# Row gathers of 128 instead of 125 table rows in the last phase of a four-layer graph network

## The reference

```python
out_deg = clip(zeros(n).at[src].add(1), 1)          # edges that leave a node
in_deg  = clip(zeros(n).at[dst].add(1), 1)          # edges that arrive at it
h       = features * (out_deg ** -0.5)[:, None]
agg     = zeros_like(features).at[dst].add(h[src])  # gather by src, add up by dst
return agg * (in_deg ** -0.5)[:, None]
```

## Time and profile before

| | |
|---|---|
| median of 3 runs | 4507.49 us |
| lowest and highest run | 4498.54 and 4508.41 us |
| the profiled execution's own time | 4501.9 us |
| its span, first to last instruction | 4500.1 us |
| busy share of the span: PE (TensorE matmul) | 97% |
| DVE (VectorE) | 91% |
| POOL (GpSimd) | 73% |
| ACT (ScalarE) | 72% |
| `l3` steady stretch, in the span | about 3855 to 4485 us |

### The profile page before, as it was taken

One profiled execution on the slowest core, in us unless ns is written; L12 is line 12 of the kernel. 1 busy time (PEld: TensorE's weight loads), 2 busy tenths in 40 slices (PEclk: granted clock), 3 DMA queues, 4 the chain that ended last, 5 costly groups with the idle time before them and its releaser, 6 DMA issues.

```text
span 4500.1 us, 107824 instructions
## 1 busy us (share of the span) xinstructions
PE 4356.4 (97%) x30591; PEld 3250.0 (72%) x30591; DVE 4096.3 (91%) x11848; ACT 3221.3 (72%) x5358; POOL 3273.1 (73%) x2516
## 2 busy tenths in 40 slices
PE   7999999999998999999999999999999998999998
PEld 5777777777775777777767777777777776666666
DVE  7999999999997999999979999997999998888888
ACT  5777777777774777777757777776777776677777
POOL 6788888888883777777747766765767675777776
PEclk8999999999999999999999999999999999999999
DMA  2111111111112322222211111111111111111111
GB/s 59 28 17 18 18 17 18 17 18 17 18 17 56 84 61 61 61 61 62 61 42 27 28 27 27 28 25 41 28 26 28 27 27 24 31 30 30 30 30 26
DMA packets 339795, 152.11 MB, mean 34 GB/s; under 512 B 250726, under 2 KB 325394, under 8 KB 339754
## 3 DMA queue, kind: packets, MB, share of 16 engines
q0 software_dynamic: 104000, 59.31, 10.3%
q1 hardware_dynamic: 235754, 92.30, 8.2%
HBM read 138.66 MB, written 10.00 MB: 33 GB/s over the span
## 4 chain that ended last, share of the span: by engine, by line
PE 87%; DVE 6%; issue 4%; ACT 1%; DMA 1%; DVEq 0%; another core or an unknown queue 0%; POOL 0%; SPq 0%; POOLq 0%; ACTq 0%
PE acc L664 40%; PE rows_ps L832 17%; PE rows_ps L759 8%; PE bank L759 6%; PE bank L848 5%; PE rows_ps L671 3%; PE eaT_ps L840 3%; PE rows_ps L747 2%; PE rows_ps L668 1%; PE eaT_ps L735 1%; DVE stationary L1325 1%; DVE raw L1349 1%; DVE one_hot L1297 1%; DVE rows_ps L1415 1%; ACT stack L1010 0%
## 5 line engine op out<-in xcount | busy, mean ns | idle before, releaser
L664 PE MATMUL acc<-one_hot,stationary 125*128 125x392 bf16 x12000 | 2334.9, 329 | 51.3 <-DVE stationary L1325 28.4
L648 POOL DMA_INDIRECT gathered<-table_l,row_numbers x1200 | 1598.6, 1332 | 449.8 <-issue 336.9
L664 PEld LDWEIGHTS acc<-one_hot,stationary 125*128 125x128 bf16 x12000 | 1150.8, 99 | 726.0 <-DVE stationary L1325 40.4
L951 ACT ACTIVATE distances<-count_hi,fields 125x392 bf16<-125x392 f16 (+1 forms) x2500 | 1223.1, 558 | 0.0
L1325 DVE TENSOR_TENSOR stationary<-mask,parts 125x1024 bf16<-125x1024 bf16 x1500 | 943.7, 683 | 0.0
L936 ACT CAST mask<-is_lo 125x1024 bf16<-125x1024 f32 x500 | 521.8, 1044 | 485.1 <-issue 293.3
L648 POOL DMA_INDIRECT fields_all<-table_l,row_numbers x500 | 645.8, 1292 | 257.4 <-issue 123.8
L1297 DVE TENSOR_SCALAR one_hot<-count_hi,fields 125x392 bf16<-125x392 f16 x2300 | 738.3, 343 | 13.6 <-issue 13.5
L1415 DVE COPY_PREDICATED rows_ps<-near_bits_now,rows_ps 125x320 f32<-125x320 int8 (+3 forms) x1600 | 580.7, 363 | 181.6 <-PE rows_ps L832 126.7
L648 POOL DMA_INDIRECT gathered<-table_l2a,row_numbers x400 | 511.5, 1279 | 263.3 <-DVE parts L1307 118.8
L648 POOL DMA_INDIRECT gathered<-table_l2b,row_numbers x400 | 511.2, 1278 | 241.3 <-DVE parts L1307 119.3
(11 more groups left out here) (220 smaller groups left out, 4704.0 us busy)
## 6 DMA issues: line engine op xcount, KB each, us to landing
near_key<-near_keys_by_chunk SPq DMA_DIRECT2D x300, 122.1 KB
gathered<-table_l,row_numbers POOLq DMA_INDIRECT x1200
fields<-edge_fields SPq DMA_DIRECT2D x500, 31.2 KB
near_key<-near_keys_by_chunk SPq DMA_DIRECT2D x100, 91.6 KB
fields_all<-table_l,row_numbers POOLq DMA_INDIRECT x500
gathered<-table_l2a,row_numbers POOLq DMA_INDIRECT x400
gathered<-table_l2b,row_numbers POOLq DMA_INDIRECT x400
ea<-in_edge_attr SPq DMA_DIRECT2D x100, 62.5 KB
```

Source lines behind the costliest of these rows:

```text
L648: pool.indirect_dma_start(out=gathered[ph][:, s, t, :], in_=table[ph], out_offset=None, in_offset=bass.IndirectOffsetOnAxis(ap=row_numbers ...
L664: mm = pe.matmul(acc[:, :], stationary[:, s, k, t, :, :].rearrange("p a b -> p (a b)"), one_hot[:, s, t, :], start=first and t == 0 and k ...
L951: ins = act.activation(distances[:, i * n:(i + 1) * n], count_hi[:, 0:n], ACT.Abs, scale=-1.0, bias=fields[:, s, k, t:t + 1].bitcast(F32))
```

## The change

The constant ROWS goes from 125 to 128. That alone only declares `row_numbers`, the gather buffers and `fields_all` with three more partitions and clears 128 partitions of `row_numbers` instead of 125. The gather then takes `rows` partitions: 128 in `l3`, 125 (EP) in the other four phases. The three further row numbers of each `l3` gather are zero, since the loader still writes only 125, so they bring row 0 of the table to partitions 125 to 127 of `gathered2`, which no instruction reads. The number of instructions on each engine and their order stay the same.

```diff
-ROWS = 125
+ROWS = 128
...
                     pool.sem_inc(ev("chunks_begun"), 1)
+                    rows = ROWS if ph == "l3" else EP
                     for t in range(far(ph, s)):
                         pool.indirect_dma_start(
-                            out=gathered[ph][:, s, t, :], in_=table[ph], out_offset=None,
-                            in_offset=bass.IndirectOffsetOnAxis(ap=row_numbers[:, s, t:t + 1], axis=0),
+                            out=gathered[ph][0:rows, s, t, :], in_=table[ph], out_offset=None,
+                            in_offset=bass.IndirectOffsetOnAxis(ap=row_numbers[0:rows, s, t:t + 1], axis=0),
                         ).then_inc(S[ph]["rows_in"][s], 16)
```

## The result

| | before | after |
|---|---|---|
| median of the runs of one comparison | 4503.01 us (4 runs) | 4676.59 us (4 runs) |
| lowest and highest | 4497.38 and 4508.41 us | 4666.19 and 4683.21 us |
| profiled execution, its own time | 4501.9 us | 4679.4 us |
| its span | 4500.1 us | 4677.6 us |

The ratio is 1.0381, with a 95% interval of 1.0368 to 1.0393: the changed kernel is 3.8% slower, 174 us. The prediction said 4472 us, with a range of 4452 to 4504, so it has the wrong sign.

What follows compares the result with a forecast made beforehand. It took `l3` to be bound by a two-chunk loop of TensorE and VectorE, stretched by GpSimd's gathers. 4501.9 - 32 - 1.2 = 4469 us, or 4474 from the median; it said 4472, range 4452 to 4504.

Steps and rivals of the forecast that it cites:

- Declaration, more rows, bytes: Three more partitions, their clearing and three more rows a gather cost nothing; 8256 bytes a gather instead of 9164.
- The gather's cost: GpSimd in `l3`: 0.5 us of writing shrinks to a third, so an undisturbed gather takes 0.87 us instead of 1.21.
- a mean under 1.0 us: Sign expected in the profile after: gathers of `l3` average under 1.0 us, those of other phases stay as before.
- The upper and lower bounds: Gather of 128 rows: 0.42 us if all shrinks with the entries, 1.31 if spreading over eleven more engines costs 0.1.
- Rival B: The gather stays as long as it is, and so do the holds: 4501 to 4508 us; chance 0.17.
- The holds on VectorE: Gathers in `l3` stretch VectorE's one-hots and casts by 31.5 us in all; about 0.33 us a chunk falls to 0.11.
- The loop: TensorE and VectorE wait on each other over two chunks of `l3`; 6.58 us a chunk falls to 6.25, gaining 32 us.
- TensorE's share of the chain: Sign expected in the profile after: TensorE has over 90% of the chain of waits in `l3`.
- GpSimd's wait for L1316: Sign in `l3`: GpSimd's wait for the freed buffer grows from 28.7 to well over 100 us.
- The end of the phase: The last chunk's cast in `l3` no longer waits for the last gather's landing: another 1.2 us gone.
- Rival C: Dealing over 16 engines costs GpSimd time, 6.72 us a chunk, so it sets the pace: 4515 to 4521 us; chance 0.13.
- Rival D: Shorter gathers whose holds fall on one-hots and casts in every chunk, gaining 0 to 8 us: 4494 to 4508; chance 0.10.

Runs made afterwards that it cites:

- e1: Changed kernel, but the gathers of `l3` take 125 rows again, with the larger declaration and clearing kept: 4504.07 us beside 4505.42 of before, ratio 0.9995.
- e5: Changed kernel, but the gathers of `l3` take 120 rows (15 engines): 4669.56 us beside 4482.15 of before.
- e8: Changed kernel, but in `l3` SyncE loads 8 keys per partition instead of 500 or so: 4664.69 us beside 4482.15 of before.
- e9: Changed kernel with a GpSimd memset of 128 x 440 behind each gather of `l3`, gathers 1.60 us apart: 4592.23 us beside 4513.0 of before.
- e10: Changed kernel, but the gathers of `l3` take 25 rows (5 engines): 4682.01 us beside 4513.0 of before.
- e2: Changed kernel, but the gathers of `l3` take 112 rows (16 engines): 4652.85 us, middle of two runs far apart, ratio 1.033.

## Why the prediction was wrong

*Declaration, more rows, bytes:* right. e1 is equal to before, and the queue moved 908 bytes a gather less, 9164 - 8256 as forecast.

*The gather's cost (1.21 to 0.87 us; the prediction's own terms, 1.21 - 0.33, give 0.88):* right in kind, a little off in size. An undisturbed gather takes 0.94 us, and the mean is 1.042, so the sign "a mean under 1.0 us" wasn't met. The runs give the scale, with the entries counted as in the prediction and the shortest gather of each: 416 entries (125 rows) 1.205 us, 288 (119 rows) 1.098, 176 (100 rows) 1.005, 144 (120 rows) 0.982, 96 (25 rows) 0.938. In these an entry costs (1.205 - 0.938) / 320 = 0.83 ns all the way down, and 0.86 us are left at none. Where every engine has rows it is 0.04 us less at the same count: 144 entries (128 rows) 0.941, 128 (112 rows) 0.927. So about 0.35 us of the 1.21 goes with the entries (416 × 0.83 ns); the 0.5 us that the prediction took was too much. The upper and lower bounds, 1.31 and 0.42, were far outside. Rival B (it stays as long) fell here, and what it cites on many descriptors doesn't hold for these counts: the measured times decide.

*The holds on VectorE:* right in direction, and not measured in size. One-hots lost 33 ns of the expected 52, the second cast 65 of 77, the first 47 of 43. That is 384 × 33 + 96 × 65 + 96 × 47 ns = 23.4 of the 31.5 us. But part of it comes from the stall: GpSimd now stands still for some 6 us in nearly every pair of chunks, and VectorE's work there runs beside no gather. The prediction also took `l2b`'s 316 ns for a one-hot without a hold, though `l2b` has the same gathers. Two one-hots of the kernel before took 0.55 us, 275 ns each, so the holds were larger than its 52 ns:

```profile
4220.05 0.55 DVE L1297 TENSOR_SCALAR one_hot<-count_hi,fields 125x392 bf16<-125x392 f16 x2 [0.29 <-issue]
```

*The loop, "what is late next is TensorE itself, as in `l2b`":* this step failed. It took for granted that the near rows are VectorE's to use as soon as TensorE has computed them, and that TensorE's own pace doesn't depend on how fast GpSimd issues gathers. Both had held in the rows I read but for 4.2 us, where gathers started no closer than 1.50 us. The gather of 0.94 us with its gap of 0.30 can start the next one 1.25 us later. In a run of eight gathers, 1.40 us apart on the mean, TensorE's progress and its signal then wait until the run is over, and VectorE waits about 5 us for it in nearly every pair of chunks. The 23 us that VectorE won are there, and 216 us of waiting lie over them. TensorE's share of the chain, forecast at over 90%, was 5.9%. My forecast of GpSimd's wait for L1316, from 28.7 to well over 100, was met (276.0), for a reason that I hadn't meant: not that GpSimd is early, but that VectorE is late.

*The end of the phase (1.2 us)* is too small to be seen beside that.

*The chances.* Rival C had the right side and the wrong reason: spreading over 16 engines cost GpSimd nothing, the gather got shorter. Rival D (shorter gathers in a worse place) came nearest in thought, since the gathers do now fall in the same place in nearly every pair of chunks, but it priced VectorE's holds alone. No rival said that GpSimd's speed is itself a load on another engine. 0.13 for slower was the sum of what I could name, and the range ended at 4504 because C was the only case beyond it.

*What stays open.* The runs show the condition (several gathers in a row, a group of four often enough, with distances down to 1.41 us or less), that it acts on TensorE (the waits show no late signal of another engine), and when it ends. They don't show what GpSimd and TensorE share, so why close gathers stop TensorE is open. I first held it to be the number of DMA engines (e5 to e8), which e9 and e10 refuted. Where between 1.41 and 1.51 us the limit lies, and whether it is sharp, wasn't measured either: the kernel before has three late signals of up to 1.4 us. Nor was it tested whether the smallest distance counts or the mean over a run (1.40 us in the changed kernel, 1.47 with 119 rows, 1.53 or more before). The price of the shorter holds wasn't measured: no run had short gathers, an even distance of 1.5 to 1.6 us and a pause that writes nothing.

## What to carry to other kernels

An engine that gets faster issues its work closer together, and that can load what the others need even if it was never the bound: before counting a gain, work out the new distance between its instructions and ask whether the trace has ever shown that distance. Where a profile shows an engine waiting for "remote" on one core, look for the instruction that sends that semaphore and compare the two times; here it led from a wait of VectorE to a stall of TensorE. And when a test by pacing comes out negative, read the distance that it reached before believing it: 1.37 us proved nothing on 1.51.

## What the runs showed of the hardware

- An indirect gather of 64-byte rows costs GpSimd 1.205 us with 416 entries, 1.098 with 288, 1.005 with 176, 0.982 with 144 and 0.938 with 96, about 0.83 ns an entry; with rows on all 16 engines it is 0.941 with 144 and 0.927 with 128. The Trainium skill ("DMA: Bandwidth & Descriptors", section "Why a DMA increments its semaphore by 16 and not by 1") lets 128 rows go to 16 engines and 125 to 5; the bytes after the change agree with the 16, 908 less a gather.
- Runs of eight gathers that start 1.24 to 1.57 us apart, 1.40 on the mean, keep VectorE waiting about 5 us for TensorE's signal, which comes 1.2 to 1.3 us after the last of them. In e2 three gathers of a group, behind a gap of 2.09 us, go with a wait of 2.64 us. With gathers of the same 128 rows at least 1.60 us apart, and a memset between them, there is no such wait (215.7 us against none).
- The number of engines, 5 or 16, makes no clear difference to that (234 and 216 us).
- A GpSimd memset of 128 x 440 (0.48 us) holds VectorE's one-hots up as a gather does: 560 ns in place of 335 with one memset for each gather.
- GpSimd's sequencer, I infer, needs about 0.7 us ahead of an indirect gather. It lies beside the gather before, unless the sequencer is made to wait: then a gap of 0.30 us became 1.02 with 4 semaphore instructions in it, and each further one added 0.08 (2.07 to 2.90 us for ten more); 1.02 - 4 × 0.08 leaves the 0.7.
